# Packing the left-over rows of all classes of a two-expert routing into full tiles and single-expert units

## The reference

```python
x = x + layernorm(attention(layernorm(x)))           # 16 heads, cumulative sums over the tokens
h = layernorm(x)
for l in range(4):
    logits = h @ router_w[l] + router_b[l]           # 4 experts
    vals, idx = top_k(softmax(logits), 2); vals /= vals.sum()
    xhat = (h - mean) * rsqrt(var + eps)
    for e in range(4):                               # only the two chosen ones count
        xe = xhat * g[l, e] + b[l, e]
        y[e] = gelu(xe @ w1[l, e] + b1[l, e]) @ w2[l, e] + b2[l, e]   # 128 -> 512 -> 128, exact gelu
    h = sum(vals[k] * (h + y[idx[k]]) for k in range(2))
x = x + layernorm(h)
```

## Time and profile before

| | |
|---|---|
| time, median of 3 runs | 1699.69 us (1698.4 to 1703.48) |
| profiled execution, its own time | 1704.1 us |
| its span | 1702.3 us |
| attention, until DVE has made the last rows | 0 to 411 us |
| first matmul of the feed-forward | 469.84 us |
| tiles of the feed-forward | 84, of 8 chunks each |
| PE busy | 1493.8 us (88%) |
| DVE, ACT, POOL busy | 1261.0, 1227.1, 979.8 us |

### The profile page before, as it was taken

The page is one execution under the profiler, slowest core; times in us unless marked ns, Lnnn a source line. Parts: engine busy times, 40 slices in busy tenths (PEclk is TensorE's granted clock), DMA queues, the critical chain, the costliest instruction groups (busy, mean ns, idle before and its releaser), DMA issues. The chain is left out here.

```text
span 1702.3 us, 38771 instructions
## 1 busy us (share of the span) xinstructions
PE 1493.8 (88%) x11652; PEld 1172.4 (69%) x11652; DVE 1261.0 (74%) x3823; ACT 1227.1 (72%) x2152; POOL 979.8 (58%) x1772
## 2 busy tenths in 40 slices
PE   7999499995099999989999999999999998888891
PEld 4666266663078888878888887878888776777771
DVE  6888388893168888878888887888888786666662
ACT  4454144441098888878888887888888788999991
POOL 2266266667425555545555554555555557888876
PEclk9999589996599999999999999999999999999996
DMA  8969831101256776655677665567766556766750
GB/s 306 399 225 397 315 126 64 49 29 35 60 197 203 232 237 206 210 176 183 200 242 229 212 209 185 182 198 241 228 218 207 184 186 163 188 183 183 189 140 7
DMA packets 194735, 324.47 MB, mean 191 GB/s; under 512 B 46445, under 2 KB 126655, under 8 KB 194528
## 3 DMA queue, kind: packets, MB, share of 16 engines
q1 hardware_dynamic: 167264, 298.46, 53.3%
q0 software_dynamic: 27264, 23.54, 6.1%
HBM read 218.99 MB, written 108.71 MB: 193 GB/s over the span
## 5 line engine op out<-in xcount | busy, mean ns | idle before, releaser
L1263 DVE TENSOR_TENSOR hl<-hg,hh 128x1024 fp32r<-128x1024 f32 x336 | 408.8, 1220 | 221.8 <-ACT hh L1196 221.8
L1190 ACT ACTIVATE hg<-ps_h,bb 128x512 f32<-128x512 f32 x672 | 437.6, 683 | 134.1 <-PE ps_h L1502 130.9
L1118 POOL DMA_INDIRECT regions<-nrow,posi x252 | 295.4, 1172 | 112.0 <-issue 62.2
L1196 ACT ACTIVATE hh<-hg 128x1024 fp32r<-128x1024 f32 x336 | 355.3, 1057 | 3.0 <-ACT hg L1190 0.3
L1500 PE MATMUL ps_h<-xTh,w1b 128*128 128x512 f32 x672 | 288.1, 429 | 2.9 <-ACT hg L1190 1.5
L1502 PE MATMUL ps_h<-xTh,w1b 128*128 128x512 f32 x672 | 265.8, 396 | 0.0
L1501 PE MATMUL ps_h<-xTl,w1b 128*128 128x512 f32 x672 | 265.5, 395 | 0.0
L1517 PE MATMUL ps_y<-hh,w2b 128*128 128x512 f32 x672 | 265.3, 395 | 0.0
L1515 PE MATMUL ps_y<-hh,w2b 128*128 128x512 f32 x672 | 264.5, 394 | 0.0
L1516 PE MATMUL ps_y<-hl,w2b 128*128 128x512 f32 x672 | 263.6, 392 | 0.0
L1531 PE MATMUL ps_q<-ir,yb 128*128 128x140 f32 (+2 forms) x1008 | 154.1, 286 | 23.1 <-DVE nrow L1300 14.3
(11 more groups left out here) (218 smaller groups left out, 2653.5 us busy)
## 6 DMA issues: line engine op xcount, KB each, us to landing
w1b<-w_split SPq DMA_DIRECT2D x168, 512.0 KB, 4.4
w2b<-w_split SPq DMA_DIRECT2D x168, 512.0 KB, 4.4
regions<-zero SPq DMA_DIRECT2D x14, 4074.0 KB, 22.8
row<-regions SPq DMA_DIRECT2D x84, 294.0 KB, 4.4
w_split<-wst SPq DMA_DIRECT2D x32, 512.0 KB, 5.5
wr<-in_L_ffn_w_dram SPq DMA_DIRECT2D x32, 256.0 KB, 4.4
x<-in_L_attn_x_dram SPq DMA_DIRECT2D x16, 256.0 KB, 4.5
out_dram<-x SPq DMA_DIRECT2D x16, 256.0 KB, 2.4
```

The source lines that it names most:

```text
L1118: g.indirect_dma_start(out=regions[layer % 2], out_offset=bass.IndirectOffsetOnAxis(ap=posi[r % 2][:, b:b + 1], axis=0), in_=nrow[r % 2][: ...
L1190: a.activation(hg[c // 2 % PAIRS][:, c % 2 * TILE:(c % 2 + 1) * TILE], ps_h[c % BANKS][:], ACT.Gelu, bias=bb[n % 4][k // FC][:, k % FC:k % ...
L1196: a.activation(hh[j % PAIRS][:], hg[j % PAIRS][:], ACT.Identity).then_inc(hi, 1)
L1263: v.tensor_tensor(hl[n][:], hg[n][:], hh[n][:].bitcast(F32), ALU.subtract).then_inc(lo, 1)
```

## The change

The order of a layer is now 21 units (NU). Sixteen of them are full tiles of 512 rows with 8 chunks ("main"), five are units of one expert with 4 chunks ("join"), 148 chunks a layer instead of 168. The order of the classes is such that neighbours share an expert. The first 11 main tiles hold rows of single stretches; main tiles 11 to 15 and the joins take rows by number from several classes. Those ten units are gathered: POOL loads their rows with four indirect DMAs each, 13 pairs ahead. A main tile that holds rows of two classes is computed with two experts; for rows that need another one, a join computes that one, `update` writes its result, multiplied by the share, into a buffer `joined`, and the main tile adds all five buffers, each with a factor of 0 or 1 (`joined_sums`). The mask `valid` is gone.

The table of the first six tiles of a layer is written after 11 main tiles of the layer before (in layer 0 at the end of attention, from the counts of the first 11 tiles); the later part of the table is written in the first pairs of the layer, with the row numbers, the joins' places and the shares' experts. Routing of the last tiles of attention has moved into the feed-forward's lists. `blank_rows(1, ...)` stands five iterations later, and b1 of layer 0 is folded in tiles 3 to 6. Weights rotate through four buffers of half a tile, rows through 8.

```diff
+JOINS = [2, 3, 1, 2, 3]
+FULL = NT - NX
-EARLY, EARLY_FROM = 6, 16
+EARLY, EARLY_FROM = 6, 11
+ORDER = [(0, p) for p in range(8)] + [(1, 0), (0, 8), (1, 1), (0, 9), (1, 2), (0, 10), (1, 3), (1, 4)] + [(0, p) for p in range(FULL, NT)]
+CHUNKS = [FC if k else KT for k in KIND]
+START = [sum(CHUNKS[:n]) for n in range(N + 1)]
...
-                    if t < ZEROS // ZBATCH:
-                        blank_rows(1, t)
+                    if 0 <= t - 5 < ZEROS // ZBATCH:
+                        blank_rows(1, t - 5)
...
+                early_counts(dve, base_early)
                 o_stats(NT - 1, 3 * NT - 2)
+                early_tiles(dve, 0)
                 make_x1(NT - 1, 3 * NT - 2)
...
+                def rows_by_number(n):
+                    l, u = layer(n), gather_of(n)
+                    pool.wait_ge(t_rows, l + 1)
+                    scattered(pool, l * NT + NT - 1)
+                    buffer_free(pool, n)
+                    for b in range(NB):
+                        at = u * NB + b
+                        g.indirect_dma_start(out=row[n % ROWBUFS][:, b, :], out_offset=None, in_=regions[l % 2],
+                                             in_offset=bass.IndirectOffsetOnAxis(ap=rowi[:, at:at + 1], axis=0),
...
+                a_place(pool, NT - 3)
...
+                a_choose(pool, NT - 2)
+                for n in range(3):
+                    rstd(n)
+                a_rows_out(pool, NT - 3, range(NB))
...
+                for j in range(TOTAL // 2 + 14):
+                    m = ENDS.get(2 * (j - 4))
+                    if main(m):
+                        identify(m)
+                    m = ENDS.get(2 * (j - 8))
+                    if routed(m):
+                        gates(tile_of(m) + NT)
+                        rows_out(tile_of(m) + NT, layer(m) + 1)
+                    if last_layer(m):
+                        add_to_output(m)
+                    n = BEGINS.get(2 * (j + 10))
+                    if n is not None and n > 3:
+                        rstd(n)
+                    m = ENDS.get(2 * (j - 7))
+                    if last_layer(m):
+                        last_rstd(m)
+                    n = BEGINS.get(2 * (j + 13))
+                    if n is not None and gathered(n):
+                        rows_by_number(n)
...
+                def shares_by_class(n):
...
+                    chained(v.tensor_tensor(gsel[q][:], sel[:, u], row[n % ROWBUFS][:, :, GATE:GATE + 2].unsqueeze(1).to_broadcast([P, 2, NB, 2]), ALU.mult))
+                    link(dve)
+                    v.reduce_sum(share[q][:], gsel[q][:], axis=AX.X).then_inc(t_share, 1)
...
+                def joined_sums(n):
+                    p, cols_ = PLACE[n] - FULL, width(n)
+                    dve.wait_ge(p_xh, n + 1)
+                    dve.wait_ge(upd, ROUND0[n])
+                    r = row[n % ROWBUFS]
+                    for q in range(NX):
+                        chained(v.scalar_tensor_tensor(r[:, :, 0:cols_], joined[q][:, :, 0:cols_], belongs[:, q, p:p + 1], r[:, :, 0:cols_], ALU.mult, ALU.add))
+                        link(dve)
...
+                def update(n, part):
+                    if part == 0 and gathered(n):
+                        shares_by_class(n)
+                        if main(n):
+                            joined_sums(n)
+                    dve.wait_ge(yt_ps, ROUND0[n] + part + 1)
...
+                def row_parts():
+                    link(dve)
+                    chained(v.tensor_tensor(row_part[:], flat_rows.unsqueeze(2).to_broadcast([P, 2 * NX * NB, NS]),
+                                            part_at[:].unsqueeze(1).to_broadcast([P, 2 * NX * NB, NS]), ALU.is_ge))
+
+                def row_values(x):
+                    link(dve)
+                    chained(v.tensor_tensor(row_gv[:], row_part[:], of_part[:, x, :].unsqueeze(1).to_broadcast([P, 2 * NX * NB, NS]), ALU.mult))
+                    link(dve)
+                    chained(v.reduce_sum(row_of[:, x, :], row_gv[:], axis=AX.X))
...
+                    for l in range(L):
+                        late = j - START[l * NU] // 2 - (8 if l else 10)
+                        if late == 0:
+                            wait(dve, t_base, (l + 1) * NT)
+                            late_counts()
+                            late_tiles(l)
+                        if late == 1:
+                            joins_of_tiles()
+                        if late == 2:
+                            row_parts()
+                            row_values(0)
+                        if late == 3:
+                            row_values(1)
+                        if late == 4:
+                            row_values(2)
+                            row_experts(l)
+                    n = BEGINS.get(2 * (j + 10))
+                    if n is not None and n > 2:
+                        stats(n)
```

## The result

The changed kernel takes 1806.07 us (median of four runs, 1803.76 to 1813.15) beside 1701.1 for the kernel before on the same chip: a ratio of 1.0625, interval 1.059 to 1.0659. It is 6% slower; the forecast was 2.3% faster, and the range ended at 1735.

A forecast was written before the change was run, and what follows sets the result against it. TensorE was taken to bound the first three layers, GpSimd's chain the last. Terms: -62 - 105 - 21 + 9 + 79 + 21 + 36 + 5 = -38 from 1704.1, scaled to 1661 us; range 1550 to 1735.

The forecast's parts named there:

- joined sums: VectorE's five additions in each gathered main tile make TensorE wait at y_tokens: 5.3 each, +79 us in three layers (30 to 107).
- gathers: GpSimd's indirect loads take 5.1 us plus 3.0 landing; four late units a layer at 3 each: +36 in three layers.
- joins: Units of half the chunks cost 6.7 us each; ScalarE's work of 7.2 adds 3 a layer: +9.
- late table: Numbers of 40 blocks add 8.7 us on VectorE over four pairs; 7 a layer, +21 in three layers (9 to 33).
- border of layers: VectorE's wait for rows of a just-written table at each layer's start goes: 3 x 6.94 = -21 us.
- Fewer chunks: A layer's 21 tiles of 13.73 us become 16 plus five units of 6.7: 35.2 a layer, -105 in three layers.
- Rival (a): The new work hides behind VectorE's free time; sums cost 30, gathers 0, table 9: 1545 us, chance 0.25.
- Rival (b): GpSimd becomes the bound; the gain is gone at a gather pitch of 1.51, at 1.85 it gives 1720 us; chance 0.24.
- The last layer: 21 rounds of 14.36 us (302) become 306, as gathers fill GpSimd's waits for ScalarE: +5 (-25 to +20).
- Start: Before the first feed-forward matmul: 39 us from the passage after attention plus 22.65 from a wait in attention: -62 (-48 to -68).
- The hole: In attention ScalarE waits 22.65 us for raw weights queued behind blanks; moving the blanks removes all (bounds 12 and 25).
- The port: VectorE operations with two SBUF inputs block GpSimd's SBUF reads; +8 us in the last layer (1669), left out of the sum.

The follow-up runs named there:

- the kernel with the three costs out: Changed kernel with joined sums left out, gathered rows replaced by 512 adjacent ones loaded by SP, and joins' y_tokens rounds and third update moved: 1588.31 us, ratio 0.9326.

## Why the prediction was wrong

The first three layers were forecast at 904.5 (48 full tiles at 13.73, 15 joins at 6.7, and the added terms) and took 997.8. Term by term, by what the removals gave back and what is left of each unit when the three large costs are out:

| first three layers, us | predicted | measured |
|---|---|---|
| joined sums | 79 | 61.5 |
| gathers | 36 | 67 |
| joins: rounds and what is left beside them | 9 | 25 + 49 = 74 |
| late table and layer 0's first tiles | 21 | 29 |
| border of layers | -21 | -17 |

- *Fewer chunks, border: right.* The plain tiles run at 13.73 plus 0.2 to 0.5, and no tile waits at the border as in the earlier trace rows (in the first three layers of the kernel before, the tile there was 6.5, 5.2 and 5.3 too long); the five at the border of the new order wait for sums and lose that wait without them.
- *Joined sums: right in place, near in size, half right in mechanism.* 3.9 to 6.1 us a tile where 5.3 was taken; a wait of 3.25 and a clock of 0.83 beside it. That 61.5 stand against 79 is in part that only 13 of the 15 waits fall into these layers. The slack of 0.2 at the place of the sums explains a good third, which spreading them took back. The rest fits the lower bound of the forecast, VectorE's throughput, and is more than its 2.0 a tile: 81 less 29 over 20 tiles is 2.6. Rival (a), which had 30 for the sums, falls with it.
- *Joins: the step that failed most.* "6.7 each, slightly under half" and 3 a layer more for ScalarE came from halving a full tile's work. A join also has its own two rounds of `y_tokens`, its own norm, transposes and updates, and does them in half of a tile's time beside the rounds of its neighbours. The rounds' order gave back 25 us in three layers. Another 49 stay even without gathers and sums and with the rounds changed, from tile 7 to tile 12, in pieces of 2 to 4. Four of these pieces hold in every one of the three layers a wait of TensorE at `y_tokens`, of 2.1, 1.4, 1.7 and 2.1 us, 7.3 of some 16 a layer (tile 7 and the second, third and fourth join). The last of them, in layer 1 of the kernel with the three costs out, ScalarE, VectorE, TensorE:

```profile
889.64 1.66 ACT L1360 ACTIVATE xh<-row,pnmr,prs 128x128 f32<-128x128 f32 x4
891.18 1.06 ACT L1382 ACTIVATE hh<-hg 128x1024 fp32r<-128x1024 f32 x1
...
892.27 1.23 DVE L1455 TENSOR_TENSOR hl<-hg,hh 128x1024 fp32r<-128x1024 f32 x1 [1.81 <-ACT hh L1382]
893.42 0.89 DVE L1518 SCALAR_TENSOR_TENSOR row<-ps_q,row 128x136 f32<-128x136 f32 x3
...
894.41 0.93 PE L1834 MATMUL ps_q<-ir,yb 128*128 128x136 f32 x6 [2.06 <-issue]
```

  ScalarE normalises a coming unit (L1360) ahead of the high part `hh`, VectorE's `rest` waits 1.81 for that, the first update of the tile before the join stands behind the `rest`, and TensorE waits for the update. In tile 6 of layer 2 of the same run the normalising stands behind that pair, and `rest` and first update follow without a wait: a join of two pairs moves the steps of the coming unit against those of the finished one. This was read at the fourth join and at tile 7 alone; what the other pieces wait for stays open.
- *Gathers: the step "5.1 and 3.0 by the median, 3 for each of four late ones".* The mean pitch is 1.63 and not 1.28, so 160 of them are 56 us more of GpSimd; 35 of these are the waits for the end of a `rest`. I counted each late unit by itself, with one scatter ahead of it; the order puts three gathers and two scatters into six pairs, and the lateness is that of the queue: 4.41 + 6.57 of VectorE at one place. Most of the measured 67 is this lateness, since other times for the same gathers gave back 48. Both could be read before: the order of the units, and the scatters' mean, (295.4 + 112.0) / 252 = 1.62 with its gaps, on the page of the kernel before:

```profile
L1118 POOL DMA_INDIRECT regions<-nrow,posi x252 | 295.4, 1172 | 112.0 <-issue 62.2
```

- *Rival (b)* had the direction and its turning point, a pitch of 1.51, which is passed; but its reason, GpSimd full, holds at best for the last layer. In the first three the other times of the gathers took back 48 with the same work.
- *The last layer: +5 forecast, +45 measured.* The sums are as forecast (19, where five waits of 4.3 were taken). The rounds of the joins, for which nothing was taken here, gave back 11. The gathers are 32, against "where GpSimd waits 1.46 for ScalarE and fill that ten times". GpSimd's timeline of the changed kernel (L1304 is the first of the additions of a tile):

```profile
1481.08 1.67 POOL L1304 DMA_INDIRECT out_dram<-fin,fidi  x1 [2.37 <-ACT fin L1402]
...
1495.66 1.65 POOL L1304 DMA_INDIRECT out_dram<-fin,fidi  x1 [2.55 <-ACT fin L1402]
...
1508.29 1.15 POOL L1268 DMA_INDIRECT row<-regions,rowi  x1 [0.77 <-issue]
...
1513.96 2.60 POOL L1304 DMA_INDIRECT out_dram<-fin,fidi  x1 [0.17 <-issue]
```

  Without a gather the additions of two tiles begin 14.6 apart, with one 18.3: of the gather's 5.3 (1508.29 to 1513.58) 1.6 lie where GpSimd would have waited for ScalarE, and 3.7 are added.
- *Start: 52.5 for 62.* The passage was right within 2. The hole was mis-sized: removing it brought 15 and not 22.65, shown alone in the kernel before; the rest is lost in earlier tiles. The three norms ahead of the last routing held; those of tiles 3 and 4 didn't, and cost 11 in layer 0.
- *The port.* The Trainium skill's page "SBUF — State Buffer", section "Who interferes with whom", was given +8 in the last layer, by joined sums that hold up GpSimd's small operations. The trace agrees: beside a joined sum GpSimd's L1286 took 0.37 us in the median of 12 cases, 0.21 in the 36 others, and in the last layer single operations of two norms took 0.88 and 2.06 where 0.23 and 1.04 are usual. Few small operations meet a sum, and little time went there. What the forecast overlooked is that VectorE's `rest`, which also has two inputs in SBUF and comes once a pair, holds up the indirect DMAs themselves: 35 us of the gathers' 200, as read above, and 48 of the scatters' 295 in the kernel before already.

## What to carry to other kernels

Price an indirect DMA by mean and gap over the whole group, (busy + idle) / count, not by the median of one, and look what the other engines do while the long ones run. When work is added to an engine that works in order, write its list for the densest stretch, here six pairs, and compare that with the time of the stretch; the share over the run (57% busy) hides a queue that ends 15 us late (36 against 20.6). Count for a half-sized unit every step that does not halve, and where its rounds fall among those of its neighbours.

## What the runs showed of the hardware

- A gather of 128 rows holds GpSimd as long as a scatter of 128 rows: 1.63 and 1.62 us with the gap (busy alone 1.25 and 1.18), landing after 3.7 us (2.5 to 5.9) for the gather and 3.3 (2.3 to 6.6) for the scatter.
- An indirect DMA that started while VectorE ran an operation with two inputs in SBUF (`rest`, 1.22 us) ended 0.84 to 1.04 us after that operation, in all 55 such gathers of the changed kernel, 63 of its 66 scatters and all 100 of the kernel before; outside, a gather took 1.00 and a scatter of the kernel before 0.97 in the median.
- Short waits can cost the clock as well: in 15 of the 17 tiles behind whose sums TensorE waited 2.5 to 4.3 us the mean granted clock was 0.83 to 0.91, in the two others (waits of 3.71 and 2.71) it stayed at 1.00. In the third join, with two waits of 6, it was 0.73. Over the whole run it was 0.903 after 0.945 before; without the three costs it was 0.946 again.
- The same attention ends at times that differ by up to 11 us between kernels that here differ only in the feed-forward (first matmul 407.4 to 418.7). Between these two, 10 of the 11 arise in the tiles that end between 92 and 196 us. Why isn't known, and whether one kernel differs as much from execution to execution wasn't traced.
